# Routing the first half of the tokens inside the last two attention groups of an AdaLN, attention and mixture-of-experts kernel

## The chip, the cores and the metric

The kernel runs on one core of one Trainium2 chip. The metric is the device time of one execution in microseconds (us), lower is better. The kernel before has a median of 799.03 us over 3 runs (798.55 to 799.05).

## What is computed

The input is 4 batches of 1024 tokens with 128 features (float32). One transformer block with adaptive layer norm runs over it:

```python
h = _layernorm(x) * (1 + ca) + sa
x = x + ga * attention(h)          # 16 heads of 8, rope, causal, softmax, output projection
h = _layernorm(x) * (1 + cb) + sb
shared_out = _expert(h, sg, su, sd)              # silu(h @ g.T) * (h @ u.T), then d
probs = softmax(h @ wr.T + rb)                   # 7 routed experts
scores, idx = top_k(probs, 2); scores = scores / scores.sum()
out = shared_out + sum_e w[..., e] * _expert(h, rg[e], ru[e], rd[e])
x = x + gb * out
```

The inner width of an expert is 352. The shifts, scales and gates (sa, ca, ga, sb, cb, gb) come from a small product per batch.

## The kernel before

**Tiling.** Tokens are handled as 32 tiles of 128, as 8 chunks n of 512 (4 tiles each, two chunks to a batch), and as two halves g of 4 chunks (2 batches). Attention runs in 16 groups ("quads", NQ = 16) of 4 heads of one batch; quads 12 to 15 are the last batch's. Each quad has 10 steps (STEPS), and a step has 3 slots (SLOTS), so 30 slots. In a step TensorE computes two pairs of scores (L1681), ScalarE takes their exp (L973, ACT), GpSimd (POOL) masks diagonal tiles (L775), and TensorE multiplies with the values two steps later (L1658).

**The ring.** Everything else that TensorE writes during attention goes through three PSUM banks in an order written out by `quad_pieces`: a list of entries, each with a slot, that TensorE writes (`ring_write`) after the score pair of that slot and VectorE (DVE) or ScalarE reads and frees (`ring_item`), strictly in this order on both sides. An entry waits until the entry three places ahead of it is freed. Kinds: row maxima of later quads ("masked", "plain", "left"), "shift" (the transposed row maxima of quad n + 1, which go by ScalarE, GpSimd and a DMA of SyncE into quad n + 1's operands), "norm" (transposed outputs of a half quad, normalised by VectorE), and in quads 14 and 15 "turn" and "project": the transposed attention output of a chunk of batches 0 to 2, copied to SBUF, and its output projection, which VectorE adds to the residual and takes the layer norm's statistics of. Quad 14 does chunks 0 to 3 from slot 9 on, quad 15 chunks 4 and 5 from slot 2 on. Row maxima of later quads end in quad 14.

**Behind attention.** The last batch's chunks 6 and 7 are turned and projected (L1710, L1766). Then, for each chunk, ScalarE normalises (L1001), TensorE turns the rows (L1722), ScalarE modulates them twice (`modulate2`: a float32 copy for the router and a high part, L1011 and L1014), VectorE subtracts the low part (`second2`, L1293), TensorE multiplies with the router (L1728) and VectorE adds the bias (`logits`). GpSimd (chunks 0 to 3) or VectorE (4 to 7) modulates the unturned rows (`modulate_rows`), which are what is scattered later. For each half VectorE then does the routing: `softmax_shift`, exp on ScalarE (`exp7`), `softmax_scale`, `ranks`, `weights`, a product on TensorE that counts (`counts`, L1736), `prefix`, `starts`, `slots`, `experts`: some 60 small operations, each waiting for the one before it (L1311 to L1400).

**Shared expert.** For each chunk TensorE computes gate and up in three pieces of the inner width (128, 128, 96; `gate_up`, L1750, 6 matmuls of 512 columns each), ScalarE takes silu (L1030), VectorE the product (`hidden`, L1416), TensorE the down product (`down`, L1758), VectorE adds it to the residual (`shared_sum`, L1420). A gate-and-up piece may be written when the hidden product two pieces ahead of it is done. The weights of the 7 routed experts are loaded and split meanwhile into a high part (`first_part`, ScalarE, L1019) and a low part (`second_part`, VectorE, L1425), through two buffers: load e waits for the low part of e - 2. The order of all this is written out per engine, and VectorE's order puts the routing steps of a half between the hidden products.

**Routed tiles.** GpSimd scatters each row to its two slots in DRAM by indirect DMA (L782, 64 in all, 32 for each half, the second half's first 8 before its tile loop and the others one by one in it). A half has 38 slot tiles of 128 rows of one expert, 76 in all. SyncE loads them (L638), TensorE transposes (L1831), computes gate and up of the tile's expert (L1843), transposes (L1864) and computes down (L1854); the parts of four tiles are in flight (`slot_step`). GpSimd scatters the result by indirect DMA (L844). TensorE begins with them when the shared expert is done and all weights are split. At the end the two results of each token are read back, added, gated and stored.

The waits at the head of the first turned rows and of the first scatters before:

```python
pe.wait_ge(s_ring_free, len(BY_DVE))             # turn_normalised(n), n < 2: attention's ring is all free
pool.wait_ge(s_hid, len(IC) + 1 + x // 2)        # scatter x of the first half paced by hidden products
```

## Time and profile before

| what | value |
|---|---|
| median of 3 runs | 799.03 us |
| profiled execution | 797.6 us, its span 795.9 us |
| busy: PE / DVE / ACT / POOL | 686.8 / 573.4 / 545.9 / 342.0 us |
| granted TensorE clock, mean | 0.947 of full |
| chain that ended last, by engine | PE 59%, DVE 18%, ACT 9%, issue 7%, DMA 3% |

The span is the time between the first and the last instruction of the profiled execution. Busy times overlap; a busy time near the length of a stretch names the engine that bounds that stretch. "PE" is TensorE's matmuls, "PEld" its weight loads. The chain of waits is followed back from the last instruction to what released each step. Positions are us from the start of the span. Attention's last two groups run from 436 to 489 us, the transition and the shared expert to 594.7, the routed tiles to 772, the rest is reading back and storing.

### The profile page before, as it was taken

What the parts mean: (1) busy time and instruction counts of PE and PEld (TensorE: products, weight loads), DVE (VectorE), ACT (ScalarE), POOL (GpSimd) and SP (SyncE); (2) the same over time, 40 slices, a digit from 0 to 9 for tenths busy, and PEclk for the clock granted to TensorE, in tenths of its full rate; (3) what the DMA queues carried; (4) which work ended last, traced back from release to release, by engine and by line L of the source; (5) the groups of instructions that cost most, each with busy time, mean ns of one, the idle gap of its engine ahead of it and who ended that gap; (6) DMA issues with size and microseconds to landing.
All of it is one profiled execution on the core that took longest, in us unless ns stands there. A gap on an engine that the chain in (4) does not pass through costs nothing.

```text
span 795.9 us, 18082 instructions
## 1 busy us (share of the span) xinstructions
PE 686.8 (86%) x5304; PEld 395.3 (50%) x5304; DVE 573.4 (72%) x2042; ACT 545.9 (69%) x1013; POOL 342.0 (43%) x551
## 2 busy tenths in 40 slices
PE   2986899999999999999999986678869989999970
PEld 1553123333333333333333434567659889999960
DVE  5797889999999999999999834574773323333543
ACT  2785259889989888989888788544325556666640
POOL 1367613232322322232322123235657887666652
PEclk9999569999999999999999999699999999999995
DMA  9246021111111111111110079202233322223425
GB/s 260 83 156 219 1 74 47 39 30 29 47 47 48 47 28 30 41 46 47 48 37 14 1 136 178 68 23 81 63 92 78 82 76 81 66 68 104 131 87 158
DMA packets 64760, 59.46 MB, mean 75 GB/s; under 512 B 10798, under 2 KB 52398, under 8 KB 64668
## 3 DMA queue, kind: packets, MB, share of 16 engines
q1 hardware_dynamic: 58924, 46.85, 23.3%
q0 software_dynamic: 4480, 9.64, 3.4%
q10 hardware_dynamic: 1264, 1.84, 0.7%
q8 instruction: 46, 0.75, 0.4%
q14 instruction: 46, 0.38, 0.2%
HBM read 33.57 MB, written 24.33 MB: 73 GB/s over the span
## 4 chain that ended last, share of the span: by engine, by line
PE 59%; DVE 18%; ACT 9%; issue 7%; DMA 3%; POOL 1%; SPq 1%; ACTq 1%; DVEq 0%; POOLq 0%
PE ps L1658 13%; PE ps L1602 10%; PE ps L1843 9%; PE ps L1681 7%; PE ps L1854 6%; DVE junk L1238 5%; ACT probs L973 5%; PE ps L1864 3%; PE ps L1758 2%; PE ps L1636 2%; DVE junk L1210 2%; PE ps L1750 2%; DMA routed_results_scratch<-y_s,s_dest 1%; PE ps L1831 1%; DVE rot L1193 1%
## 5 line engine op out<-in xcount | busy, mean ns | idle before, releaser
L973 ACT ACTIVATE probs<-ps 128x1024 f32<-128x1024 f32 (+1 forms) x320 | 285.5, 941 | 34.5 <-PE ps L1681 32.1
L1210 DVE CUSTOM_DVE_ANT_0 junk<-ps,tri 128x512 f32<-128x512 f32 (+3 forms) x512 | 218.5, 487 | 13.9 <-PE ps L1602 11.6
L1602 PE MATMUL ps<-ka,qa 61*128 61x256 bf16 (+3 forms) x788 | 186.7, 325 | 10.0 <-DVE rowmax L1210 3.0
L775 POOL TENSOR_SCALAR_AFFINE_SELECT probs<-probs 128x512 f32<-128x512 f32 x128 | 79.7, 634 | 191.8 <-ACT probs L973 191.8
L1658 PE MATMUL ps<-probs,v 128*32 128x512 f32 (+3 forms) x1536 | 157.7, 498 | 1.3 <-POOL probs L775 1.1
L1681 PE MATMUL ps<-qa,ka 64*128 64x512 bf16 (+3 forms) x768 | 144.6, 331 | 7.7 <-ACT probs L973 5.6
L1602 PEld LDWEIGHTS ps<-ka,qa 61*128 61x128 bf16 x788 | 53.0, 95 | 159.8 <-DVE rowmax L1210 80.4
L844 POOL DMA_INDIRECT routed_results_scratch<-y_s,s_dest x76 | 76.2, 1003 | 41.0 <-issue 35.0
L782 POOL DMA_INDIRECT slot_rows_scratch<-rows,slot x64 | 64.1, 1001 | 56.6 <-DVE slot L1393 30.1
L1243 DVE TENSOR_REDUCE leftmax<-ps 128x1 f32<-128x512 f32 x120 | 78.4, 686 | 8.5 <-PE ps L1602 8.5
L1532 DVE TENSOR_TENSOR hid_s<-sg,ps 128x352 f32<-128x352 f32 x76 | 39.6, 521 | 46.2 <-ACT sg L1087 46.0
L1854 PE MATMUL ps<-wd,hidT 128*128 (+1 forms) x456 | 64.3, 277 | 5.8 <-ACT hidT L1105 5.8
L1525 DVE TENSOR_TENSOR h_lo<-ps,h_hi 128x128 fp32r<-128x128 f32 x76 | 22.2, 291 | 59.7 <-ACT h_hi L1080 59.3
L1854 PEld LDWEIGHTS ps<-wd,hidT 128*128 128x128 f32 (+1 forms) x456 | 60.6, 192 | 7.4 <-issue 7.3
L1658 PEld LDWEIGHTS ps<-probs,v 128*32 128x32 f32 x1536 | 33.8, 108 | 54.5 <-issue 49.3
L1681 PEld LDWEIGHTS ps<-qa,ka 64*128 64x128 bf16 x768 | 42.5, 94 | 33.4 <-ACT probs L973 21.2
L1087 ACT ACTIVATE sg<-ps 128x352 f32<-128x352 f32 x76 | 35.2, 463 | 33.8 <-PE ps L1843 32.0
L1096 ACT ACTIVATE y_s<-ps,s_weight 128x128 f32<-128x128 f32 x76 | 27.9, 367 | 33.5 <-PE ps L1854 25.4
L1238 DVE CUSTOM_DVE_ANT_0 junk<-ps,above 128x256 f32<-128x256 f32 x136 | 49.3, 419 | 0.0
L749 POOL TENSOR_TENSOR mrest<-mneg,mparts 32x128 f32<-32x128 f32 x16 | 6.7, 417 | 92.7 <-ACT mparts L936 92.7
L1843 PE MATMUL ps<-w_hi,h_hi 128*128 x152 | 45.3, 380 | 1.2 <-issue 1.1
L1210 DVE DVE_READ_ACCUMULATOR2_ANT rowmax<- 128x1 f32 x512 | 42.6, 83 | 0.1
(195 smaller groups left out, 1168.4 us busy)
## 6 DMA issues: line engine op xcount, KB each, us to landing
slot_rows_scratch<-cst SPq DMA_DIRECT2D x1, 5396.0 KB, 36.1
srow<-slot_rows_scratch SPq DMA_DIRECT2D x76, 71.0 KB
k_parts_scratch<-qk_parts SPq DMA_DIRECT2D x12, 320.0 KB, 2.7
ka<-k_parts_scratch SPq DMA_DIRECT2D x32, 120.0 KB
q_parts_scratch<-qk_parts SPq DMA_DIRECT2D x12, 256.0 KB, 2.6
qa<-q_parts_scratch SPq DMA_DIRECT2D x32, 96.0 KB
ka<-k_parts_scratch SPq DMA_DIRECT2D x32, 80.0 KB
xs<-in_x SPq DMA_DIRECT2D x4, 512.0 KB, 9.4
```

The source lines that it names most:

```text
L775: nc.gpsimd.affine_select(out=p, in_=p, compare_op=ALU.is_ge, fill=0.0, base=0, pattern=[[0, HQ], [1, T]], channel_multiplier=-1).then_inc ...
L782: nc.gpsimd.indirect_dma_start(slot_d, bass.IndirectOffsetOnAxis(ap=slot[:, k, t:t + 1], axis=0), rows[:, t, :], None).then_inc(s_scatter[ ...
L844: nc.gpsimd.indirect_dma_start(y_d, bass.IndirectOffsetOnAxis(ap=s_dest[:, d:d + 1], axis=0), y_s[:, j, :], None).then_inc(s_y_out[j], 16)
L973: nc.scalar.activation(probs[(n * NS + s) % 4][:, 2 * h:2 * h + 2, 0:UNTIL[s] - FROM[s]], ps[:, 2 * h:2 * h + 2, FROM[s]:UNTIL[s]], ACT.Ex ...
L1210: last = V.tensor_tensor_reduce(out=junk[:, bank - 5, at:at + w], in0=ps[:, bank, at:at + w], in1=tri[:, CH - w:CH], scale=1.0, scalar=LOW ...
L1238: last = V.tensor_tensor_reduce(out=junk[:, bank - 5, cols], in0=ps[:, bank, cols], in1=above[:, h, q - CG, :], scale=1.0, scalar=LOW, op0 ...
L1243: last = V.reduce_max(leftmax[m][:, row, q - CG:q - CG + 1], ps[:, bank, :], AX.X)
L1602: last = MM(ps[:, bank, at:at + w], qa[m][g0:g0 + KS, c0 + q * T:c0 + (q + 1) * T], ka[m][g0:g0 + KS, d0 + k0:d0 + k0 + w], start=True, st ...
L1658: last = MM(ps[VW * h:VW * (h + 1), 4, q0:CH], v4[m][:, k, h, :], probs[(n * NS + s) % 4][:, h, p0:p0 + CH - q0], start=begins, stop=ends ...
L1681: last = MM(ps[:, 2 * pair + g, at:at + CH - q0], ka[m][g * HG:(g + 1) * HG, pair * KW + kb * T:pair * KW + (kb + 1) * T], qa[m][g * HG:(g ...
L1843: last = MM(ps[:, 1 + 2 * t2 + g, 0:NI], ht[:, t2, :], wt[:, bass.ds(e, 1), g, :], start=(k == 0), stop=(k == 2))
L1854: last = MM(ps[:, 6, 0:D], hidT[0:w, t2, c, :], wd[0:w, bass.ds(e, 1), c, :], start=(c == 0), stop=(c == len(IC) - 1))
```

## The change

The entries of `quad_pieces` for quads 14 and 15 are now two tables. In quad 14 the turns and projections of chunks 0 to 3 go to slots 19 to 29. VectorE then takes the variance of half 0 (16 tiles; before, of 24 tiles behind attention) and normalises its 16 tiles itself, with a square root that ScalarE takes at step 2 of quad 15 (`deviation(0)`). In quad 15 three new kinds of entries route half 0: "rows" (transposed rows, modulated by VectorE into hT), "router" (logits) and "counts"; VectorE does `softmax_shift`, `softmax_scale`, comparisons, `ranks`, `weights`, `prefix`, `starts`, `slots` and `experts` between and at these entries, ScalarE the exp at step 7. Turns and projections of chunks 4 and 5 move to slots 17 to 22. GpSimd modulates the rows of half 0 at steps 5 and 6 of quad 15.

Behind attention the rows of chunks 0 to 3 are turned after their modulation, so ScalarE only copies the high part. The shared expert begins when the last batch's residual is added. Half 1 is routed later in VectorE's order, in pieces of a generator between the hidden products of chunks 4 to 7, with the four `modulate_rows` of half 1 among them; `shared_sum(4)`, `(5)` and `(6)` now stand right behind the first hidden product of chunks 5, 6 and 7. Down of chunk 3 and router 7 stand ahead of gate and up of chunk 4. Second-half scatters: 12 ahead of the tile loop instead of 8; the first half's are not paced any more. All loops over slot tiles are written out, and the first half's results are read back three loads earlier.

```diff
+FIRST_HALF = [(19, "turn", 0), (20, "turn", 1), (21, "project", 0), (23, "turn", 2), (24, "project", 1),
+              (26, "turn", 3), (27, "project", 2), (29, "project", 3)]
+SECOND_HALF = [(9, "rows", 0), (10, "rows", 1), (11, "router", 0), (12, "rows", 2), (13, "router", 1), (14, "rows", 3),
+               (15, "router", 2), (16, "router", 3), (17, "turn", 4), (18, "turn", 5), (20, "project", 4), (22, "project", 5),
+               (28, "counts", 0)]
-    units = {NQ - 2: range(4), NQ - 1: range(4, 2 * (B - 1))}.get(n, ())
...
+    late = {NQ - 2: FIRST_HALF, NQ - 1: SECOND_HALF}.get(n, ())
+    plan += [(slot, kind, n, None, u) for slot, kind, u in late]
...
+        AHEAD = 12
+        ROWS_TURNED = {u: slot for slot, kind, u in SECOND_HALF if kind == "rows"}
...
                 for s, tiles in enumerate(STEPS):
+                    for u in range(GC) if n == NQ - 1 else ():
+                        if s == (ROWS_TURNED[u] // SLOTS) + 2:
+                            modulate_rows(u)
...
-                pool.wait_ge(s_hid, len(IC) + 1 + x // 2)
...
+                    if s == 2 and n == NQ - 1:
+                        deviation(0)
+                    if s == 7 and n == NQ - 1:
+                        exp7(0)
...
+                if n < GC:
+                    nc.scalar.activation(h2_hi[:, n * CH:(n + 1) * CH], ps[:, TURN[u], :], ACT.Copy).then_inc(s_h2_hi, 1)
+                    return
...
             normalise(7)
             first_part(1)
+            first_part(2)
             silu(3)
             modulate2(7)
-            first_part(2)
+            first_part(3)
+            exp7(1)
             silu(4)
-            exp7(1)
-            first_part(3)
+            first_part(4)
             silu(5)
-            first_part(4)
+            first_part(5)
             silu(6)
-            first_part(5)
+            first_part(6)
             silu(7)
-            first_part(6)
...
+                elif kind == "counts":
+                    incl = prefix(0, bank)
+                    end = starts(0, incl)
+                    slots(0, incl, bank)
+                    dve.sem_inc(s_ring_free, 1)
+                    experts(0, end)
...
+            for x in range(len(RING_PIECES)):
+                ring_item(x)
+                done = RING_PIECES[x][1:]
+                if done == ("project", NQ - 2, None, GC - 1):
+                    variance(GTILES[0], s_var2)
+                    scale2(0)
+                    dve.wait_ge(s_v4, NQ)
+                    for n in range(GC):
+                        normalise(n)
+                elif done == ("router", NQ - 1, None, GC - 1):
+                    V.memset(beats[:], 0.0).then_inc(s_beats, 1)
+                    softmax_shift(0)
+                elif done == ("project", NQ - 1, None, GC):
+                    softmax_scale(0)
+                    dve.wait_ge(s_beats, 1)
+                    beaten(0, range(NE))
+                elif done == ("project", NQ - 1, None, GC + 1):
+                    ranks(0)
+                    weights(0)
...
+            def route_second():
+                softmax_scale(1)
+                yield
+                beaten(1, range(4))
+                yield
+                beaten(1, range(4, NE))
+                yield
+                ranks(1)
+                yield
+                weights(1)
+                modulate_rows(4)
+                yield
+                modulate_rows(5)
+                incl = prefix(1, GROUPED)
+                yield
+                modulate_rows(6)
+                end = starts(1, incl)
+                yield
+                modulate_rows(7)
+                yield
+                slots(1, incl, GROUPED)
+                yield
+                experts(1, end)
+                yield
+                yield
...
             softmax_shift(1)
             second2(7)
+            shared_sum(3)
+            next(routing)
+            hidden(4, 0)
+            next(routing)
+            hidden(4, 1)
+            next(routing)
+            next(routing)
+            hidden(4, 2)
+            next(routing)
             hidden(5, 0)
-            modulate_rows(7)
+            shared_sum(4)
+            next(routing)
             hidden(5, 1)
-            softmax_scale(1)
-            ranks(1)
+            next(routing)
             hidden(5, 2)
-            shared_sum(4)
-            weights(1)
+            next(routing)
             hidden(6, 0)
-            second_part(3)
-            incl = prefix(1)
+            shared_sum(5)
+            next(routing)
             hidden(6, 1)
-            end = starts(1, incl)
+            second_part(4)
             hidden(6, 2)
-            shared_sum(5)
-            slots(1, incl)
+            next(routing)
             hidden(7, 0)
-            second_part(4)
-            experts(1, end)
+            next(routing)
+            shared_sum(6)
             hidden(7, 1)
             second_part(5)
             hidden(7, 2)
-            shared_sum(6)
             second_part(6)
             shared_sum(7)
...
-            turn_normalised(7)
-            gate_up(4)
+            turn_rows(7)
             down(3)
             router(7)
+            gate_up(4)
             gate_up(5)
             down(4)
-            counts(1)
+            pe.wait_ge(s_sel, GRP)
+            group_counts(1, GROUPED).then_inc(s_prefix, 1)
```

## Rows read from the trace of the kernel before

**Rows 1.** Busy time by stretch: stretch, length, then busy us (xinstructions) per engine, granted clock.

```profile
463.48:483.60 20.12, 18.45 (x172) 7.58 (x176) 6.57 (x23) 17.18 (x21) 3.88 (x7) 1.00 1.09 199
502.90:529.90 27.00, 18.21 (x90) 14.57 (x90) 20.01 (x74) 11.35 (x21) 3.11 (x4) 0.82 0.01 4
547.50:594.70 47.20, 38.61 (x241) 32.71 (x239) 34.04 (x94) 15.46 (x23) 26.62 (x27) 0.97 0.27 79
```

**Rows 2.** TensorE's timeline, last attention group: start, us, line, form [idle before, releaser].

```profile
463.48 0.61 PE L1681 MATMUL ps<-qa,ka 64*128 64x512 bf16 x4 [1.68 <-DMA qa<-mparts]
465.01 0.66 PE L1621 MATMUL ps<-eye,xn 128*128 128x128 f32 x4
...
473.77 1.16 PE L1627 MATMUL ps<-wo_gated,oT 128*128 128x128 f32 x8
```

**Rows 3.** ScalarE's timeline, last attention group: step 2, step 7, table load.

```profile
467.81 1.94 ACT L973 ACTIVATE probs<-ps 128x1024 f32<-128x1024 f32 x2
...
479.82 1.02 ACT L973 ACTIVATE probs<-ps 128x1024 f32<-128x1024 f32 x1 [0.72 <-PE ps L1681]
...
484.98 1.28 ACT L995 ACT_TABLE_LOAD   x1
```

**Rows 4.** VectorE's timeline: eight normalisations at the start, the last norm.

```profile
10.09 2.14 DVE L1165 TENSOR_SCALAR xn<-xs,mean,rstd 128x128 f32<-128x128 f32 x8
...
489.40 0.29 DVE L1263 TENSOR_TENSOR xn<-ps,recip 128x128 f32<-128x128 f32 x1
```

**Rows 5.** VectorE's busy time in each step of the second half's routing.

```profile
567.95:571.87 3.92, 3.73 (x18) 1.00 0.16 56
573.07:574.46 1.39, 1.27 (x6) 1.00 0.12 33
576.07:578.08 2.01, 1.85 (x11) 1.00 0.42 102
578.68:580.70 2.02, 1.77 (x12) 1.00 0.12 42
581.90:585.05 3.15, 2.81 (x13) 1.00 0.00 0
586.48:587.47 0.99, 0.92 (x4) 1.00 0.29 90
```

**Rows 6.** Chain of waits through the shared expert: start, us, what.

```profile
503.07 4.31 PE ps L1750 x12
...
515.47 2.87 PE ps L1750 x6
...
528.82 0.79 PE ps L1728 x8
...
531.59 1.35 ACT rows L1001 x4
...
547.69 4.04 PE ps L1758 x24
...
566.03 0.70 DVE rows L1406
...
585.82 1.63 PE ps L1750 x6
587.44 2.69 PE ps L1758 x24
```

**Rows 7.** Timeline of GpSimd and VectorE where their passes overlap.

```profile
495.33 1.18 POOL L793 TENSOR_TENSOR rows<-rows,mod_rows 128x512 f32<-128x512 f32 x1 [0.18 <-POOL rows L789]
495.50 1.04 DVE L1132 TENSOR_TENSOR part_a<-stats 128x8 f32<-128x8 f32 x1
```

**Rows 8.** GpSimd's timeline: two result scatters, 19 tile steps apart.

```profile
604.45 1.00 POOL L844 DMA_INDIRECT routed_results_scratch<-y_s,s_dest  x1 [1.62 <-issue]
...
657.04 1.00 POOL L844 DMA_INDIRECT routed_results_scratch<-y_s,s_dest  x1 [0.16 <-issue]
```

**Rows 9.** TensorE's busy time and matmuls of L1843 in a stretch of routed tiles.

```profile
662.00:733.00 71.00, 40.57 (x199) 31.36 (x200) 1.00 0.24 69
```

393 lines of the change are left out of this document (175 added, 218 removed).

## The prediction

> **What bounds the kernel now.** I read the busy time by stage first [rows 1], then the timelines of the engines in the last attention group [rows 2 to 4], the chain of waits through the shared expert [rows 6], and GpSimd's timeline and TensorE's pace in the routed tiles [rows 8, 9]. Four stretches matter. (a) The last attention group's score window is full for two engines: of 20.1 us TensorE is busy 18.5 and ScalarE 17.2, VectorE only 6.6 [rows 1]. (b) Attention ends at 489.69 us, when VectorE has normalised the last output [rows 4]; I call this t0. (c) From 502.9 to 529.9 VectorE is the bound (20.0 of 27 us): it does the first half's routing between the pieces of the shared expert, and TensorE sits idle 6.8 us before the piece at 515.47 [rows 1, 6]. (d) From T = 547.5, the end of chunk 3's gate and up products, to 594.7, the end of the shared expert, TensorE is busy 38.6 of 47.2 us [rows 1]. The routed tiles follow: GpSimd paces the first ones, TensorE the others [rows 8, 9]. The change takes work out of (c), puts it into (a), and reorders (d).
>
> **Prices.** Four transposes 0.6 us, a projection 1.1 [rows 2], a router 0.8, a gate-and-up piece 1.45 (its row of 1.63 runs to the last drain), a down product 2.7, a VectorE pass over 128x512 0.6 to 0.7 [rows 6]. One sixteenth of normalise on VectorE 0.26 (eight in 2.14, rows 4). A table switch on ScalarE 1.28 [rows 3]. Routing of one half on VectorE: scale, comparisons and ranks 3.9, weights 1.35, prefix 2.0, starts 2.0, slots 3.15, experts 1.0 [rows 5].
>
> **Part 1, group 14 (next to last).** The turns and projections move behind the transposition of the next group's row maxima. That shift then starts some 3.4 us earlier and 3.4 us more of TensorE work lies behind it, so the 1.68 us wait for its DMA [rows 2] is covered. TensorE is otherwise full, its work is the same: **-1.7 us**.
>
> **Part 2, group 15 (last).** I count from its first scores (463.48 before). Before, the second steps' exps end at 6.3 [rows 3] and t0 is at 26.2. After:
> - ScalarE's step 2 ends at about 5.7; then table load and square root to 7.2. VectorE scales to 7.7 and normalises 16 tiles to 11.9 (16 x 0.26), all before it takes any further ring entry. TensorE has reached slot 9 at about 5.4 and waits there for the first four tiles, to 8.9; behind this wait in its queue stand score pair 1 of step 3 and so ScalarE. ScalarE has to load the exp table again (1.28).
> - The first router needs VectorE's modulated copy, which stands behind the 16 tiles: 12.7.
> - From there TensorE has score pairs, value products, 4 more transposition and router entries, turns 4 and 5 and projections 4 and 5, and is the bound: adding entry after entry, step 5 starts at 17.6, step 6 at 21.4, step 7 at 24.5, step 7's exps end at 26.8 (before: 17.4, rows 3).
> - Only then ScalarE does the router's exp (27.1), which VectorE waits for: scale and comparisons to 29.7, then the norm and projection entries held up behind them (0.6 + 1.5) to 31.8, ranks 33.0, weights 34.3. TensorE waits for the ranks with its counts product at slot 28, and the last three value products (3 x 1.0) stand behind it: 33.8 to 36.8, copy and transposes to 38.1. VectorE does prefix, starts, slots and experts (8.15) to 42.4, and only then the last norm: t0 at 43.0.
> So t0 comes 43.0 - 26.2 = **+16.8 us** later. The lower bound needs no TensorE queue at all: the chain behind step 7's exps (the router's exp 0.3, then 3.9 + 2.1 + 1.35 + 8.15 + 0.6 = 16.1 of VectorE) starts no earlier than 17.4 + 2.6 for the two table loads, which gives 36 and +10.
>
> GpSimd's modulation of the first half (8 passes of 1.18) runs from about 9.6 to 20 in this group; its own masks are needed later, cost none. But a VectorE pass of two SBUF operands that began under such a pass took 1.04 us where its like takes 0.2, and ended with GpSimd's [rows 7]. Whether normalise, with one SBUF operand, waits too is not in the trace: between 0 (it is not held) and 4.0 us (its last 8 tiles held until GpSimd's first four passes are over, and the first router with them). I take **+2.0**, the middle, since only a pass of another kind shows it.
> The Trainium skill (GPSIMD Engine Reference, Key points) says that GpSimd contends with VectorE instructions of two SBUF inputs or in a 2-port mode. The trace agrees for the first kind (1.04 us against 0.2). By that rule the term would be 4.0 and the time 2 us more than I give.
> The Trainium skill (ScalarE: Activation LUTs, What ACT_TABLE_LOAD costs) gives about 2.66 us for each change of set, load and drain, and tells to group calls by set, which speaks against a square root between exps. The trace shows the load, 1.28, right behind the last exp, with no gap for a drain. By the page the stretch would be 2.8 us longer and the sum some 2 us more.
>
> **Part 3, from t0 to chunk 2.** Before: 40.2 us (489.69 to 529.9). After, from t0: turns of the last batch to 1.15, first two row turns to 2.35, projections to 4.4, and VectorE's two low parts and two residual sums to 6.2: gate and up of chunk 0 start at 6.2 instead of 13.4 [rows 6]. Their first two pieces take 4.3 as before (half clock at first). Silu's table is in place at 9.8, the first hidden product at 11.1, the third piece runs at 11.15 without the 6.8 us wait. Then ScalarE is next: it normalises chunk 4 (1.64; the chain shows 1.35 of such a step, rows 6) before row turn 4, to 15.1, and has modulation and normalise again ahead of chunk 1's silu, to 18.8. Down of chunk 0 ends at 24.2, router 25.0, chunk 2 starts at 25.65: **-14.5 us**.
> Chunks 2 and 3 keep their pace, 17.6 us before; one more weight split (0.8) ahead of chunk 3's silu, a 0.4 us slow clock less: **+0.4**.
>
> **Part 4, from T to the end of the shared expert (before 47.2).** Gate and up of chunk 4 now come behind down of chunk 3 and its router: start T + 7.6 instead of T + 5.3. The four modulations of rows (1.4 each; only one was in this stretch) and all routing of the second half go between the pieces, and three residual sums are placed ahead of hidden products: VectorE waits there for a down product that TensorE issues only after the piece released by the hidden product before. From T: hidden (4,0) 11.3, (4,1) 12.85, (4,2) 15.5 behind the ranks, (5,0) 18.8 behind weights and a modulation; piece and down to 23.0; sum, modulation, prefix, (5,1) 27.6; modulation and starts, (5,2) 31.5; (6,0) 33.5; piece and down to 37.7; sum and slots (3.15), (6,1) 42.1. The last expert weights are loaded only after the split that follows (43.0), and ScalarE converts them ahead of chunk 7's silu: (7,0) at about 48.7. Piece and down to 52.85, sum, two hiddens and a split 55.6, down and sum 59.3. So 59.3 - 47.2 = **+12.1 us**. It is a chain of VectorE and TensorE in turns; the DMA in it I took as 3 to 4 us.
>
> **Part 5, routed tiles.** GpSimd scatters 12 second-half tiles ahead instead of 8 (15.1 us from T + 41.5, over at T + 56.6; this is covered by 2.7 us, and each us beyond would count in full), so 20 instead of 24 ride in its tile loop. Before, 19 steps ran at (657.04 - 604.45) / 19 = 2.77 us while a tile of TensorE, six such matmuls, takes 71.0 x 6 / 199 = 2.14 [rows 8, 9]. Four steps fewer x 0.63: **-2.5 us**. Unrolled loads, the read of results three tiles earlier, the order of allocations and the unpaced first scatters (40 us, over long before their rows are read): 0, since the same queues do the same bytes; -1 to +2 for where the result read collides.
>
> **Sum.** -1.7 + 16.8 + 2.0 - 14.5 + 0.4 + 12.1 - 2.5 = +12.6. Span 795.9 + 12.6 = 808.5; the profiled run was 797.6, so 1.7 lies around the span: 810.2. The median of the runs is 1.4 above the profiled one; I forecast **811**. Bounds of the terms: part 2 from +10 to +21, part 4 from +6 to +15.
>
> **Rivals.**
> *Not slower after all (0.13), about 791.* VectorE's idle time in group 15 (13.5 of 20.1 us) takes the routing in, so that the group grows only by TensorE's added entries (6.5 us less the 1.6 idle, 4.9), and half of part 4 overlaps: -1.7 + 4.9 - 14.5 + 6 - 2.5 = -7.8. For it: that idle time. Against it: order. It decides at one place, the router's exp behind step 7; the routing tail would have to end before ScalarE's last copy.
> *A draw (0.07), about 799:* the same, with part 2 at its lower bound of +10 and part 4 at +6.
> *Half clock in part 4 (0.17), about 823.* TensorE would be busy about 25 of the 46 us from T + 13 on. The piece at 515.47, behind 6.8 us of idleness, took 2.87 against 1.63, and a down product at 547.69 took 4.04 against 2.69 [rows 6]. Seven such pieces and three downs on the chain: 7 x 1.24 + 3 x 1.35 = 12.7 more. Against it: the piece at 585.82, which also stood behind a wait for a hidden product, ran at full clock [rows 6].
> *My forecast* has 0.63. The change does what it says, since all of it is program order; the only thing outside is the padding write, whose start does not move back.
>
> **Range and chances.** What this kernel's measurement can tell from no change is about 0.2%, 1.6 us. Forecast's bounds and part of the half-clock case: 800 to 823. Faster 0.12, same 0.07, slower 0.81.
>
> **What would show it.** Right: in the last group ScalarE has two more table loads, TensorE a gap of over 3 us ended by VectorE's normalise, and one ended by the ranks; t0 near 505; no gap of 6.8 us in chunk 0; chunk 2 some 26 us behind t0; gaps of 3 to 4.5 us in chunks 5 to 7, ended by hidden products; shared end near 608. Wrong: t0 before 498 (part 2's queue is not the bound), or less than 52 us from T to the end (part 4 overlaps).

## The result, and the profile after

| | kernel before | kernel after |
|---|---|---|
| median (4 runs each) | 798.79 us | 827.14 us (822.93 to 827.50) |
| ratio to before | | 1.0344, 95% interval 1.0310 to 1.0378 |
| span of the profiled execution | 795.9 us | 825.2 us |
| granted TensorE clock, mean | 0.947 | 0.923 |

The change makes the kernel 28 us slower. The direction is the one forecast, the size is 16 us above the 811 and 4 us above the range's end of 823.

The page of the kernel after, its head, two engines' busy time and the granted clock in 40 slices:

```profile
span 825.2 us, 17955 instructions
...
PE 704.4 (85%) x5320; PEld 405.4 (49%) x5320; DVE 584.2 (71%) x2062; ACT 538.6 (65%) x994; POOL 341.7 (41%) x550
...
PEclk9997579999999999999999958799887999999995
```

Before, TensorE was busy 686.8 us. Now it is busy 17.6 us longer for 16 more matmuls: the same work at a lower clock, and the clock row shows where, in slices 24 to 26 and 29 to 31 (of 20.6 us each): the last attention group, the stretch behind it and the second half of the shared expert.

The stretches of the prediction, as windows of the kernel after (start:end, length, busy time of each engine with its number of instructions, granted clock, DMA share, GB/s). They run from the last group's first scores to t0, to gate and up of chunk 2, to T, to the end of the shared expert, to the end:

```profile
core 0: us, PE busy (x) PEld busy (x) DVE busy (x) ACT busy (x) POOL busy (x), PEclk, DMA share, GB/s
462.19:516.84 54.65, 37.68 (x257) 19.14 (x256) 34.69 (x117) 22.56 (x27) 16.42 (x19) 0.78 0.67 112
516.84:543.86 27.02, 21.78 (x117) 18.18 (x117) 11.80 (x33) 14.12 (x25) 20.62 (x22) 0.81 0.36 107
543.86:562.46 18.60, 13.41 (x75) 10.68 (x74) 7.62 (x12) 10.52 (x20) 9.33 (x10) 0.97 0.21 62
562.46:626.42 63.96, 46.23 (x241) 38.01 (x239) 35.00 (x96) 14.66 (x22) 16.19 (x22) 0.82 0.14 43
626.42:825.20 198.78, 168.50 (x1216) 162.30 (x1216) 76.36 (x173) 108.91 (x380) 125.21 (x243) 0.93 0.32 91
```

Against before, term by term:

| stretch | before | after | difference | forecast |
|---|---|---|---|---|
| up to the last group's first scores | 463.48 | 462.19 | -1.3 | -1.7 |
| last group, to t0 | 26.2 | 54.65 | +28.4 | +18.8 |
| t0 to gate and up of chunk 2 | 40.2 | 27.0 | -13.2 | -14.5 |
| chunk 2 to T | 17.6 | 18.6 | +1.0 | +0.4 |
| T to the end of the shared expert | 47.15 | 63.96 | +16.8 | +12.1 |
| routed tiles to the end | 201.3 | 198.8 | -2.5 | -2.5 |
| sum | | | +29.2 | +12.6 |

Two terms carry the miss: +9.6 in the last group and +4.7 from T on. The others are off by 2.3 in all.

TensorE's timeline in the last group of the kernel after, the lines ahead of which it stood idle for over 2 us and some of the routers (start, length, line, output and inputs, count, idle time before and what ended it):

```profile
471.88 0.63 PE L1664 MATMUL ps<-eye,rows 128*128 128x128 f32 x4 [3.73 <-DVE rows L1403]
...
479.45 1.84 PE L1668 MATMUL ps<-wr,hT 128*128 128x7 f32 x8 [4.37 <-DVE hT L1230]
...
484.20 1.87 PE L1668 MATMUL ps<-wr,hT 128*128 128x7 f32 x8
...
490.81 1.06 PE L1668 MATMUL ps<-wr,hT 128*128 128x7 f32 x8
...
506.61 1.14 PE L1635 MATMUL ps<-sel,cst 128*128 128x112 f32 x4 [2.46 <-DVE sel L1310]
...
516.90 1.97 PE L1753 MATMUL ps<-eye,xn 128*128 128x128 f32 x8 [3.83 <-DVE xn L1249]
```

VectorE's and then GpSimd's lines beside them. VectorE's sixteen normalising operations take 7.96 us, not 4.2, and GpSimd's first passes of modulation lie under them:

```profile
470.62 7.96 DVE L1403 TENSOR_SCALAR rows<-xs,mean,rstd 128x128 f32<-128x128 f32 x16 [0.15 <-DVE nbias L1121]
```

```profile
472.69 1.19 POOL L746 TENSOR_TENSOR rows<-rows,mod_rows 128x512 f32<-128x512 f32 x1 [2.86 <-PE ps L1664]
474.06 1.28 POOL L750 TENSOR_TENSOR rows<-rows,mod_rows 128x512 f32<-128x512 f32 x1 [0.18 <-POOL rows L746]
475.31 1.23 POOL L746 TENSOR_TENSOR rows<-rows,mod_rows 128x512 f32<-128x512 f32 x1
```

ScalarE's, from the third step's exps on, shows the chain's head: exps to 468.45, then the square root with its two table loads, then VectorE:

```profile
466.51 1.94 ACT L955 ACTIVATE probs<-ps 128x1024 f32<-128x1024 f32 x2
468.47 1.28 ACT L931 ACT_TABLE_LOAD   x1
469.76 0.21 ACT L931 ACTIVATE rstd<-rstd 128x16 f32<-128x16 f32 x1
469.99 1.28 ACT L955 ACT_TABLE_LOAD   x1
```

From T on, some of TensorE's waits for hidden products, and the last down product, which took 5.49 us where the four ahead of it took 2.84 each:

```profile
591.55 0.50 PE L1786 MATMUL ps<-h_hi,ws_hi 128*128 128x512 f32 x1 [4.22 <-DVE hid L1389]
...
607.24 0.80 PE L1786 MATMUL ps<-h_hi,ws_hi 128*128 128x512 f32 x1 [4.53 <-DVE hid L1389]
...
614.59 2.84 PE L1794 MATMUL ps<-wds_gated,hid 128*128 128x128 f32 x24
...
620.20 5.49 PE L1794 MATMUL ps<-wds_gated,hid 128*128 128x128 f32 x24 [2.77 <-DVE hid L1389]
```

and VectorE's residual sums in the same stretch, placed behind the first hidden product of the next chunk; each waits for a down product that TensorE issues only behind the next piece (a third such sum, at 617.47, waits 4.39 us):

```profile
586.94 0.69 DVE L1393 TENSOR_TENSOR xs<-xs,ps 128x512 f32<-128x512 f32 x1 [4.39 <-PE ps L1794]
...
602.75 0.69 DVE L1393 TENSOR_TENSOR xs<-xs,ps 128x512 f32<-128x512 f32 x1 [5.38 <-PE ps L1794]
```

### The profile page after: what moved, and what is told of

Read it like the earlier page. It is cut to its first block and busy times, and to the rows that moved or that the text cites. A ratio compares the mean times of both kernels' runs of the same rounds, so it can differ in the third digit from the quotient of the medians.

```text
span 825.2 us, 17955 instructions
## 1 busy us (share of the span) xinstructions
PE 704.4 (85%) x5320; PEld 405.4 (49%) x5320; DVE 584.2 (71%) x2062; ACT 538.6 (65%) x994; POOL 341.7 (41%) x550
## 3 DMA queue, kind: packets, MB, share of 16 engines
q10 hardware_dynamic: 1264, 1.84, 0.7%
## 5 line engine op out<-in xcount | busy, mean ns | idle before, releaser
L955 ACT ACTIVATE probs<-ps 128x1024 f32<-128x1024 f32 (+1 forms) x320 | 285.5, 940 | 49.5 <-PE ps L1724 47.2
L1183 DVE CUSTOM_DVE_ANT_0 junk<-ps,tri 128x512 f32<-128x512 f32 (+3 forms) x512 | 218.4, 487 | 14.1 <-PE ps L1627 11.8
L1701 PE MATMUL ps<-probs,v 128*32 128x512 f32 (+3 forms) x1536 | 160.4, 507 | 0.3 <-ACT outT L943 0.3
L1724 PE MATMUL ps<-qa,ka 64*128 64x512 bf16 (+3 forms) x768 | 146.3, 334 | 6.6 <-ACT probs L955 6.3
L1701 PEld LDWEIGHTS ps<-probs,v 128*32 128x32 f32 x1536 | 34.2, 110 | 55.0 <-issue 50.7
L1786 PE MATMUL ps<-h_hi,ws_hi 128*128 128x512 f32 (+1 forms) x48 | 23.4, 488 | 22.4 <-DVE hid L1389 21.3
```

Of the source, the lines that this page charges most:

```text
L955: nc.scalar.activation(probs[(n * NS + s) % 4][:, 2 * h:2 * h + 2, 0:UNTIL[s] - FROM[s]], ps[:, 2 * h:2 * h + 2, FROM[s]:UNTIL[s]], ACT.Ex ...
L1183: last = V.tensor_tensor_reduce(out=junk[:, bank - 5, at:at + w], in0=ps[:, bank, at:at + w], in1=tri[:, CH - w:CH], scale=1.0, scalar=LOW ...
L1701: last = MM(ps[VW * h:VW * (h + 1), 4, q0:CH], v4[m][:, k, h, :], probs[(n * NS + s) % 4][:, h, p0:p0 + CH - q0], start=begins, stop=ends ...
L1724: last = MM(ps[:, 2 * pair + g, at:at + CH - q0], ka[m][g * HG:(g + 1) * HG, pair * KW + kb * T:pair * KW + (kb + 1) * T], qa[m][g * HG:(g ...
```

## The experiments

My theory after the result: in the last group, (a) GpSimd's modulation slows VectorE's normalising, (b) TensorE idles ahead of the rows and then runs at half clock, (c) the routing's tail (`starts`, `slots`, `experts`) delays the last norm; from T on, (d) the place of the residual sums. "Last group" below is from its first scores to t0 in each kernel's own trace.

The runs were taken in groups, and each group has its own measure of the kernel before. For e1 to e8, e17 and e18 that took 799 to 800 us. For e9 to e16 it took 833 to 835 us, and those are compared only among themselves and by stretches of the last group. There is no trace of the kernel before from these. The record gives the chip of each group by a number, and number 8 stands beside 833 and 834 us (e9 to e13) as well as beside 799 us (e17 and e18), so whether the 833 us belong to a chip or to a time is open.

### e1: TensorE kept busy

```diff
+                    keep_busy(m, bank, 14 if what == 0 else 0)   # ahead of the wait for rows 0
...
+                    keep_busy(m, bank, 18 if what == 0 else 0)   # ahead of the wait for router 0
```

The 32 extra matmuls write into a bank that the next entry overwrites; nothing of the computation is left out.

> The changed kernel with 32 matmuls added whose results nobody reads: 14 ahead of the wait for the first normalised rows and 18 ahead of the first router, each of 512 columns into the bank that the entry behind them overwrites. They fill the two idle times of TensorE (3.7 and 4.4 us) in the last group. Theory clock: these idle times bring the granted clock to half, which costs some 7 us in the group (a router takes 1.8 us where it took 0.8). Then routers ahead of step 6 take 0.8 to 1.0 us, the end of attention comes some 7 us earlier and the time is 819 to 822. Rival: VectorE's queue sets the group's end and the slow matmuls are hidden behind it: the matmuls run faster, but the time stays within 2 us of 827, or rises by as much as the added matmuls overrun the gaps.

Median 825.59 us (819.85 to 827.66), ratio 1.0342 [1.0318, 1.0365]. TensorE's lines ahead of the first router, profiled execution:

```profile
466.12 3.18 PE L1641 MATMUL ps<-qa,ka 64*128 64x512 bf16 x14
...
472.17 4.05 PE L1641 MATMUL ps<-qa,ka 64*128 64x512 bf16 x18
...
477.50 1.06 PE L1674 MATMUL ps<-wr,hT 128*128 128x7 f32 x8 [1.27 <-DVE hT L1230]
```

In this execution, the fastest of four, routers take 1.06 and the last group 48.6 us in place of 54.65. The stretch from the first router to the first scores of step 6 holds the same 80 matmuls in both kernels, and TensorE is busy through all of it. In the kernel after, and in e1:

```profile
479.45:493.70 14.25, 14.25 (x80) 9.53 (x81) 4.61 (x12) 4.70 (x5) 4.72 (x4) 0.62 1.15 180
```

```profile
477.50:486.93 9.43, 9.43 (x80) 6.52 (x81) 4.60 (x12) 4.69 (x5) 4.74 (x4) 1.00 1.17 173
```

So the lower clock costs 4.8 us in this stretch, with contention and square root as they were, and e1's group is 6.0 us shorter in all. As a cure the filling isn't shown: the median of 825.59 is the rival's, within 2 us of 827. The time follows the mean clock from execution to execution, with the filling (819.85 us at 0.940, 827.66 at 0.925) and without it (the kernel after: 822.93 at 0.934, 827.50 at 0.924). So the runs show what the half clock costs, not what brings it.

### e2: GpSimd's modulation behind the normalising

```diff
+                pool.wait_ge(s_xn2, GC)
                 pool.wait_ge(s_ring, RING_INDEX["rows", NQ - 1, None, n] + 1)
```

> The changed kernel with one wait more: GpSimd begins to modulate the first half's rows in the last group only when VectorE has normalised all 16 tiles. Theory contention: GpSimd's passes hold VectorE's normalisation (8.0 us for what takes 4.2). Then the 16 tiles take 4.2 us, the first router starts 3.8 us earlier, and TensorE's second idle time shrinks to under 1 us: time 823 if the clock falls all the same, down to 816 if it stays full. Rival: normalise is slow for a reason of its own (two engines and a write of strided rows): its 16 tiles still take about 8 us, and the time is 827 or more.

Median 819.05 us (815.51 to 826.10), ratio 1.0236 [1.0189, 1.0284]. VectorE's line:

```profile
470.85 4.19 DVE L1404 TENSOR_SCALAR rows<-xs,mean,rstd 128x128 f32<-128x128 f32 x16 [0.15 <-DVE nbias L1122]
```

Normalising takes 4.19 us, so (a) holds: the contention costs 3.8 us. The median fell by 8.1 us and lies within the theory's 816 to 823. The profiled execution, though, was the slowest of four and kept routers of 1.84 and 1.87, all four of them, and its last group is only 1.9 us shorter: its trace shows the shorter normalising and not where the median's 8 us come from.

### e3: the routing's tail behind the last norm

```diff
-                    end = starts(0, incl)
-                    slots(0, incl, bank)
...
-                    experts(0, end)
...
+            end = starts(0, kept[0])      # behind the last norm
+            experts(0, end)
...
+            slots(0, kept[0], None)       # behind hidden(0, 1)
```

> The changed kernel with the end of the first half's routing moved on VectorE: starts and experts stand behind the last norm of attention, slots behind the second hidden product of chunk 0; only prefix and a copy of the counts stay ahead of the last norm. Theory queue: the last norm stands behind 8 us of routing and TensorE waits for it, so attention ends about 6 us earlier and the time is about 821 to 822.5 (some of the moved 6 us lands on the chain of chunk 0). Rival: the work is only moved and VectorE bounds the next stage as well: the time stays within 1.5 us of 827.

Median 822.68 us, ratio 1.0285 [1.0245, 1.0325]; last group 51.1 us, 3.6 shorter, and t0 to the first down product 21.7 in place of 23.1. So (c) is worth some 4.5 us, about what the theory gave (821 to 822.5). The intervals of e3 and of the kernel after (1.0310 to 1.0378) overlap a little, so the size is rough; the shorter group stands in the trace.

### e4 and e6: residual sums later, and 8 scatters ahead

```diff
             hidden(5, 0)
-            shared_sum(4)
...
             hidden(5, 2)
+            shared_sum(4)
```

and likewise sums 5 and 6 behind `hidden(6, 2)` and `hidden(7, 2)`. Prefix, starts, slots and the last modulation of rows move back with the sums, by one or two hidden products; they stay in this stretch. e6 is e4 with `AHEAD = 8`.

> The changed kernel with VectorE's order in chunks 5 to 7 altered: the residual sums of chunks 4, 5 and 6 stand behind the third hidden product of the next chunk, as before, and prefix behind the sum of chunk 4; the routing steps and row modulations are the same and stay in this stretch. Theory order: three times VectorE waits 4.4 to 5.4 us for a down product while TensorE waits for VectorE's hidden product, so of the stretch from chunk 3 to the end of the shared expert (63.9 us, 47.2 before) 9 to 12 us go: time 815 to 819. Rival: the stretch is long because there is more routing in it and because of TensorE's half clock: it shrinks by 3 us at most, time 824 or more.

> The kernel with VectorE's sums of the shared expert's chunks 4 to 6 behind the third hidden product of the next chunk, now with 8 in place of 12 tiles of first results laid down ahead of the routed weights. Theory (the routed stage was 5 us longer in that kernel since the 12 scatters end later than the shared expert): the routed stage is back at 199 to 201 us, the shared expert's second half stays at 46 to 48 us, and the time is 808 to 811 us. Rival (the routed stage begins with the table of weights and destinations, which depends on the routing's last steps, not on the scatters): the routed stage stays at 203 to 204 us and the time at 813.

e4: median 813.49 us, ratio 1.0183 [1.0147, 1.0220]. The window from T to the end of its shared expert:

```profile
562.50:609.00 46.50, 38.13 (x239) 32.03 (x238) 34.72 (x95) 14.34 (x22) 7.94 (x8) 0.98 0.16 48
```

46.5 us in place of 63.96: (d), the order of VectorE's steps with the sums at its head, is the whole +16.8 of this stretch, more than the 9 to 12 us expected. The sums now wait 0.55 us, not at all and 1.37 us in place of 4.39, 5.38 and 4.39. TensorE's busy time fell by 8.1 us (38.13 against 46.23, clock 0.98 against 0.82) and its idle time by 9.4 (8.4 against 17.7): the waits, and the lower clock that came with them, in about equal parts. Some 5 us came back in the routed tiles (203.7 against 198.8), since the twelve scatters, the first at 598.93, ended at 614.31, behind the shared expert's end at 608.6, and the table of weights and destinations came only then (GpSimd):

```profile
613.35 0.96 POOL L782 DMA_INDIRECT slot_rows_scratch<-rows,slot  x1 [0.30 <-issue]
614.32 0.20 POOL L808 COPY s_weight<-srow 128x1 f32 x1
```

e6: median 811.24 us (810.48 to 817.04), routed tiles 202.1. The gain of 2 us lies inside the spread of both, and 202.1 lies between the theory's 199 to 201 and the rival's 203 to 204, so the scatters' part stays undecided.

### e5: no contention, and the first idle stretch filled

e2's edit and e1's first 14 matmuls.

> The kernel after with two things in its last attention group: GpSimd's modulation of the rows begins only behind VectorE's sixteen normalising operations, and 14 extra matmuls of 512 columns are issued ahead of the wait for the first rows (their results are overwritten; nothing of the computation is left out). Theory (the half clock in the last group follows TensorE's idle stretch of 3.7 us ahead of the rows; that and the collision of VectorE with GpSimd are the missing 10 us): normalising takes 4.2 us, the first router matmuls 0.8 to 1.1 us in place of 1.87, the last group to the end of its last normalisation 44 to 46 us in place of 54.7, and the time 815 to 818 us. Rival (the clock falls there for another reason than that one idle stretch): routers still at 1.8, the group at 51 to 53, and 819 to 826 us as without the extra matmuls.

Median 824.29 us (820.22 to 826.66). Routers 1.83 and 1.87 in spite of it, last group 49.5:

```profile
470.86 0.66 PE L1670 MATMUL ps<-eye,rows 128*128 128x128 f32 x4 [0.63 <-DVE rows L1404]
...
474.74 1.83 PE L1675 MATMUL ps<-wr,hT 128*128 128x7 f32 x8 [1.57 <-DVE hT L1231]
```

Filling the 3.7 us does not keep the clock: behind waits of 0.63 and 1.57 us TensorE ran its routers at half clock for some 10 us. The rival holds in the routers and the time, and as a cure the filling falls; the group is between the two forecasts (44 to 46, and 51 to 53). That its median is 5 us above e2's is not explained; their intervals, 1.0271 to 1.0360 and 1.0189 to 1.0284, overlap.

### e7 and e8: the costs undone together

e7 is e2, e3 and e6 in one, with `second_part(4)` and `(5)` one step earlier. e8 moves on top of that the turns and projections of chunks 4 and 5 ahead of the rows. VectorE then normalises behind the residual sum of chunk 5 and takes the routing's steps from scale to weights behind the first norm, and ScalarE takes the router's exp at step 6:

```diff
-SECOND_HALF = [(9, "rows", 0),
...
+SECOND_HALF = [(0, "turn", 4), (1, "turn", 5), (2, "project", 4), (4, "project", 5), (9, "rows", 0),
...
```

> The kernel after with four things set right at once: GpSimd's modulation behind the normalising; the first half's starts and experts behind the last normalisation and its slots behind the shared expert's first hidden product; VectorE's sums of chunks 4 to 6 later, with the gated products of chunks 4 and 5 one step earlier; 8 scatters ahead in place of 12. Theory (the costs stand in different stages and add): minus 4 to 8, minus 4, minus 14 and minus 3 us from 827 give 796 to 800 us. Rival (what is saved in the last group is given back as idle TensorE and a lower granted clock in the shared expert, since each stage then waits for VectorE): 803 to 810 us.

> As the kernel with the four things set right, and in the last attention group TensorE turns and projects tiles 4 and 5 in its first slots, ahead of the first half's rows, while the softmax, comparisons and ranks of the first half come on VectorE behind the last tile's normalisation. Theory (VectorE's work of the routing's first steps stood between the last group's start and the end of its normalisation, and TensorE's idle stretch ahead of the rows is filled with work that was to be done anyhow): the last group takes 33 to 40 us in place of 54.7, and the time is 788 to 795 us, under the kernel before. Rival (the routing's steps only move behind the normalisation, where counts and the shared expert's hidden values wait for VectorE): 796 to 803 us, no better than the kernel with four things alone.

e7: median 799.31 us (10 runs), ratio 1.0027 [1.0004, 1.0051]. The singles had saved 8, 4.5 and 13.7 us, e6's scatters 2; together they save 28, so they add, and the theory's 796 to 800 holds. The windows of e7's last group and of its stretch from T on:

```profile
460.88:503.87 42.99, 33.25 (x257) 16.21 (x256) 25.68 (x93) 22.55 (x27) 14.80 (x17) 0.88 0.89 143
549.00:596.03 47.03, 38.91 (x241) 32.73 (x239) 35.46 (x96) 14.65 (x22) 17.69 (x20) 0.96 0.22 64
```

The last group is still 16.8 us above before's 26.2, and what is won behind it (some 13 us up to chunk 2) no more than pays for that: with these costs gone, the change is a draw.

e8: median 798.03 us (10 runs), ratio 0.9981 [0.9968, 0.9994], last group 40.2. That is 0.2% under the before of its own group. e18 below, the same kernel with its scatters paced, has the same median and a ratio of 0.9995, so a gain over before isn't shown. It is the rival's time rather than the 788 to 795 of the theory: TensorE's idle stretch ahead of the rows stayed (3.74 us, rows at 474.67), since the exps and the square root behind them moved back with the projections.

### e9 to e16: where the square root stands

```diff
                 for s in range(NS):
+                    if s == 1 and n == NQ - 1:
+                        deviation(0)
...
-                    if s == 2 and n == NQ - 1:
-                        deviation(0)
```

e10, e11 and e15 are the kernel after with this edit alone, e16 adds e2's, e12 is e7 with it, e9 and e13 are e8 with it, and e14 is the kernel after itself on the same chip as e15 and e16.

> The kernel with projections first, with ScalarE's square root for the first half's normalisation ahead of the second step's exps of the last group (in its idle stretch of 3.0 us) in place of behind the third step's. Theory (with the square root there, VectorE normalises right behind the residual sum of tile 5, some 4 us earlier, and TensorE's idle stretch of 3.74 us ahead of the rows and the half clock behind it go): normalising starts near 469.5 in place of 473.4, routers at 1.06 or less, the last normalisation 3 to 5 us earlier, the time 793 to 796 us, under the kernel before by 0.4% or more. Rival (the two table loads delay the exps that TensorE's value products wait for, or the group is bound by TensorE alone): the last normalisation at most 1 us earlier, the time 797 to 799.

> The kernel after with this one edit: ScalarE's square root for the first half's normalisation ahead of the second step's exps of the last group in place of behind the third step's. Theory (what came on top of the prediction in the last group is a chain from this square root through normalising to the rows, the idle TensorE ahead of them and its half clock): normalising starts 2.5 to 3.5 us earlier, the idle stretch ahead of the rows shrinks from 3.7 to under 1.5 us, the last normalisation comes 3 to 6 us earlier, and the time is 820 to 824 us. Rival (GpSimd's modulation and the queue behind the routing's steps set the group's end whatever the square root does): the last normalisation 0 to 2 us earlier and the time at 824 to 827.

> The same edit of the kernel after as before (square root ahead of the second step's exps), once more since the earlier run's chip showed pauses of ScalarE of up to 12 us in the shared expert. Theory (the 9.8 us that its trace of the last group shows are gained in the time too): the last group 44 to 47 us, the time 816 to 820 us where before takes 799, or the ratio to the kernel before 1.021 to 1.027. Rival (TensorE's half clock falls elsewhere in that group or in the shared expert and gives it back): 822 to 826 us, ratio 1.029 to 1.034.

> The kernel with four things set right (modulation later, routing's tail behind the last normalisation, sums later, 8 scatters ahead), and the square root ahead of the second step's exps. Theory (normalising starts 3 to 4 us earlier, and the last group was bound from there): the last normalisation 3 to 4 us earlier than in that kernel, the ratio to the kernel before 0.994 to 0.998, under before. Rival (with the contention gone, the square root's place is no longer what binds the group, and the two table loads delay the exps instead): ratio 1.000 to 1.004, as without the edit.

> The kernel with the projections of tiles 4 and 5 first and the square root ahead of the second step's exps, once more, beside the others on one chip. Theory of the first trace of it (TensorE idles 0.2, 0.75 and 1.57 us in place of 3.74, yet runs at half clock over 477 to 490, which takes back what was gained): the last group 42 to 44 us, the ratio to before 1.000 to 1.006. Rival (that half clock was one execution's): the last group 37 to 39 us and a ratio of 0.992 to 0.996.

> The kernel after itself, as the measure for the two kernels beside it on the same chip. If this is a chip on which the kernel before takes 799 us: 823 to 828 us, last group 53 to 55 us. If it is the one on which before takes 833: the pauses of ScalarE in the shared expert are those of that chip, not of the square root's place, so the trace shows them here too, and the time is 880 to 885 us (the 874 with the square root earlier, plus up to 10); if they come from the square root's place, it is below 865.

> The kernel after with the square root ahead of the second step's exps. Theory (the last group's 9.9 us arrive in the time): 7 to 10 us below the kernel after on the same chip. Rival (half clock or waits in the shared expert give them back): 0 to 4 us below it.

> The kernel after with the square root ahead of the second step's exps and GpSimd's modulation behind the normalising. Theory (normalising collides with GpSimd only for 0.8 us once the square root is early, 4.98 against 4.19 us, so the two edits remove one and the same cost): 0 to 1.5 us below the kernel with the square root alone. Rival (the costs add): 4 to 8 us below it.

| kernel | median | ratio to before | last group |
|---|---|---|---|
| e14, after | 886.10 us | 1.0628 [1.0607, 1.0648] | 54.55 |
| e15, square root early | 873.74 | 1.0472 [1.0448, 1.0495] | 44.6 |
| e10, e11, the same | 873.39, 874.01 | 1.0496, 1.0466 | 44.8, 44.7 |
| e16, and no contention | 874.22 | 1.0474 [1.0451, 1.0497] | 43.4 |
| e12, e7 with it | 853.71 | 1.0245 [1.0199, 1.0292] | 42.7 |
| e9, e13, e8 with it | 854.56, 855.69 | 1.0263, 1.0238 | 43.6, 41.9 |

Against e14, this one edit takes 9.96 us off the last group, and they arrive: the median falls by 12.4 us (the profiled spans, 882.1 and 871.7, differ by 10.4). That is more than the theory's 7 to 10 and far from the rival's 0 to 4. e10 and e11 show the same group; their times, expected for a before of 799 us, decide nothing. The last group of e14 and of e15:

```profile
461.03:515.58 54.55, 37.67 (x257) 19.29 (x256) 34.71 (x117) 22.56 (x27) 16.52 (x19) 0.78 0.65 113
```

```profile
460.94:505.53 44.59, 35.13 (x257) 16.60 (x256) 31.82 (x117) 22.55 (x27) 16.30 (x19) 0.84 0.77 138
```

Of the 10 us, 2.5 are TensorE's busy time (clock 0.78 to 0.84) and 7.4 its idle time. VectorE and the first router in e15:

```profile
465.55 4.98 DVE L1403 TENSOR_SCALAR rows<-xs,mean,rstd 128x128 f32<-128x128 f32 x16 [0.15 <-DVE nbias L1121]
```

```profile
466.86 1.08 PE L1724 MATMUL ps<-qa,ka 64*128 64x384 bf16 x8 [2.15 <-ACT probs L957]
...
471.46 0.66 PE L1664 MATMUL ps<-eye,rows 128*128 128x128 f32 x4
```

Normalising starts 3.8 us earlier in the group (4.6 in place of 8.4 behind the first scores) and is over at 470.53, before GpSimd's modulation starts at 471.40, so nothing collides but one masking pass of 0.80 us. TensorE never waits for the rows; it waits 2.15 us for the delayed exps instead. e16 confirms it: with e2's edit too, normalising takes the same 4.98 us and the time stays (874.22 against 873.74), so the two edits remove one and the same contention, as the theory of e16 had it. In e12 the edit gives 0.3 us (42.7 against e7's 43.0), and on e8 it makes the group longer (43.6 and 41.9 against 40.2), with two or three of the four routers at 1.84 to 1.88, though TensorE's longest wait ahead of them was 1.57 us. For the last group the theories of e9 and e12 fell and their rivals hold; e13's theory for it (42 to 44 us) is nearly met. How the times of e12, e9 and e13 would stand to e7 and e8 side by side wasn't measured.

The traces of e9 to e16 show something that the others don't: with the 32 scatters of the first half under way, ScalarE and VectorE stop for up to 22 us (e13) with nothing in the trace that ends the stop. ScalarE in e14, the first two silu of the shared expert, which in the kernel after ran without a wait:

```profile
545.29 0.60 ACT L1010 ACTIVATE sgs<-ps 128x512 f32<-128x512 f32 x1 [8.45 <-remote]
...
557.23 0.60 ACT L1010 ACTIVATE sgs<-ps 128x512 f32<-128x512 f32 x1 [11.33 <-remote]
```

They come without the square root's edit too, so they aren't its doing, as e14's expectation had it for a before of 833 us (its 886.10 lies 1 us above the 880 to 885 given). "remote" is what the trace prints where it finds no releaser. From t0 to T, e14 takes 74.9 us where the kernel after takes 45.6: about half of the 57 us between their spans. What makes the engines stop is open.

### e17 and e18: the scatters paced again

```diff
                 if t == 0:
                     pool.wait_ge(s_slot, k + 1)
+                pool.wait_ge(s_hid, len(IC) + 1 + x // 2)
```

> The kernel after with the first half's scatters paced again by the hidden products, as in the kernel before. If the step 'unpaced scatters cost nothing' was right: where the kernel before takes 799 us the time is that of the kernel after, 823 to 828 us (ratio 1.031 to 1.037); where it takes 833 us the pauses of ScalarE stay and the ratio is 1.060 to 1.065. Rival (32 scatters in one go keep instructions or data of the other engines waiting): the pauses in the shared expert's first chunks shrink or move, and the ratio falls below 1.05 on such a chip, or by 2 us or more on the other kind.

> The kernel with the projections first and the three costs undone, with the first half's scatters paced again. If unpaced scatters cost nothing: ratio to the kernel before 0.997 to 1.000 where that takes 799 us, as without the pacing, and 1.02 to 1.027 where it takes 833. Rival: ratio below 1.01 on a chip of the second kind, and 0.990 to 0.996 on one of the first.

e17 (the kernel after with it): 825.39 us, ratio 1.0335 [1.0318, 1.0352]. e18 (e8 with it): 798.03 us (12 runs), ratio 0.9995 [0.9973, 1.0016]. No gain where before takes 799 us: the prediction's zero for the unpaced scatters holds there. No paced run was taken where before takes 833 us, so whether the pauses go with the pacing stays open.

## Why the prediction was right and wrong

**Right: direction and the balance.** Part 1 (-1.7, measured -1.3), part 3 (-14.5, -13.2), chunks 2 and 3 (+0.4, +1.0) and part 5 (-2.5, -2.5) hold within 1.3 us each. For part 5 no run isolates the reason given, the four scatters fewer in the loop, so there only the number is shown. The main argument, that the last group takes up the routing end to end behind step 7's exps and the tail ahead of the last norm, is what the trace shows: TensorE waits 2.46 us for the ranks and 3.83 us for the last norm. "Not slower after all" (0.13) decides where the prediction put it, at the router's exp, which comes 38.1 us behind the first scores. The draw (0.07) is reached only with the costs undone (e7). Of what was named as a sign of error, "t0 before 498" and "less than 52 us", neither came.

**Wrong: the size of part 2.** Against its own positions, counted from the first scores:

| | forecast | after | e1's trace | e15 |
|---|---|---|---|---|
| normalising starts, ends | 7.7, 11.9 | 8.4, 16.4 | 8.4, 16.4 | 4.6, 9.6 |
| first router | 12.7 | 17.3 | 17.2 | 11.7 |
| first scores of step 6 | 21.4 | 31.5 | 26.6 | 21.9 |
| t0 | 43.0, and 2.0 for the contention | 54.65 | 48.6 | 44.6 |

Of the 11.65 us between 43.0 and 54.65, 4.6 stand ahead of the first router. 3.8 of them are the contention, for which I had taken the middle of 0 and 4.0 where the upper end was true; the rest is mostly the square root, 0.7 us later than forecast. Another 5.5 come between router and step 6, for which I had 8.7 us and the kernel needs 14.25. e1's trace, with the same order at full clock, needs 9.43: so 4.8 of the 5.5 are the half clock, and 0.7 my sum of TensorE's entries. The last 1.55 are spread behind it, and 1.1 of them are gone in e1's trace too. In all, by these two traces, the half clock is worth 6.0 us and the contention 1.8 more than the 2.0 that I gave it: 7.8 of part 2's miss of 9.65.

The step that failed is that I priced a half clock as a rival of part 4 only. In part 2 I wrote down a TensorE wait of 3.5 us (to 8.9; it was 3.73) and went on at the full-speed prices of rows 2, though rows 6 show a piece of 2.87 us in place of 1.63 behind a long wait. That this wait brought the half clock isn't shown: e7's trace has the same 3.73 us and routers at full clock, and e5's has only short waits and slow ones. What makes the clock fall stays open. e15's t0 lies near the forecast's 45.0, but by another course: its normalising starts 3.1 us ahead of the forecast's.

**The contention.** Normalising took 7.96 us under GpSimd's passes and 4.19 without them (e2). This is an operation with one SBUF operand of 128 columns; the Trainium skill (GPSIMD Engine Reference, Key points) names VectorE instructions of two SBUF inputs or in a 2-port mode. By that rule, as the prediction read it for this operation, the term was 4.0: the trace agrees, with 3.8, and so does the sum that the prediction gave beside its own. In which mode the operation ran no trace shows.

**The table loads.** Square root and two loads took 468.47 to 471.27, 2.8 us, with the first load right behind the last exp. The Trainium skill (ScalarE: Activation LUTs, What ACT_TABLE_LOAD costs) gives about 2.66 us for each switch, which would make it 5.5; the measurement decides, and 1.28 a load was the right price. The Trainium skill's advice to group calls by table set (ScalarE: Activation LUTs, Table sets: the hidden batching unit) bears here all the same: the two loads cost ScalarE 2.6 us, but the place of the square root cost 10 us in the group, 3.0 of them contention. I counted the delay of VectorE by them and didn't ask what the same root would do ahead of the second step's exps.

**Part 4: right chain, clock left out.** From T, hidden products (4,0), (5,0), (6,0) and (7,0) were forecast at 11.3, 18.8, 33.5 and 48.7 and start at 11.8, 19.4, 34.2 and 49.9. Up to there the chain of residual sum, hidden product and piece is as worked out, 0.5 to 1.2 us late, and e4 shows that the order with the sums ahead is all of it. Of the 4.7 us above the forecast the other 3.5 arise behind (7,0); 2.6 of them are the last down product at half clock (5.49 us against 2.84). The rival "half clock in part 4" (0.17, +12.7) is half true: TensorE's busy time from T on rose from 38.6 to 46.2 us, but (7,0) stood only 1.2 us late, so of these 7.6 us little more than the last down product shows in the length of the stretch. The row at 585.82, which I held against it, was one piece behind one wait.

**The range.** With both of its upper bounds (part 2 at +21, part 4 at +15) the sum is -1.7 + 21 - 14.5 + 0.4 + 15 - 2.5 = +17.7, which gives 817; the end of 823 came from the half-clock rival of part 4. The measured +28.4 lies outside part 2's own bound of +21: that bound held the whole contention and nothing for the clock. Two figures don't follow from the prediction's own terms either: 810.2 + 1.4 is 811.6, not 811, and t0 by its sum stands at 463.5 - 1.7 + 43.0 + 2.0 = 506.8, where its signs say 505. Neither changes what is said above.

## What to carry to other kernels

When a chain crosses three engines inside a stretch that was full, look for its earliest link and ask what an earlier place would do: here one square root's place in ScalarE's order was worth 10 us, contention and idle TensorE included, and 0.3 us on e7, where the contention was gone and the clock full. A consumer that waits for a producer which the consumer's own output feeds (a residual sum ahead of the hidden product that releases the next piece) cost twice here, 9.4 us as waiting and 8.1 us as lower clock. And where you write down an idle stretch on TensorE, give the matmuls behind it at half speed a price and a chance of their own in every part, not in one; these runs don't tell which stretch will bring it.

## What the runs showed of the hardware

- A VectorE tensor_scalar over 128x128 f32 with one SBUF operand, sixteen in a row: 4.19 us alone (e2), 7.96 under GpSimd tensor_tensor passes of 128x512 (after), 4.98 with a masking pass of GpSimd under it (e15).
- The same 80 matmuls took 14.25 us at a mean granted clock of 0.62 and 9.43 at 1.00, with TensorE busy throughout in both (after and e1).
- The granted clock does not follow from the idle time just before alone: behind 3.73 us of idleness routers took 1.03 in e7's trace, behind 1.57 us they took 1.83 in e5's. In e9's trace TensorE was busy for all of the 13 us from 477 to 490 at a granted clock of 0.50. Executions of one kernel differ with it: e1's four had clocks of 0.925 to 0.940 and times of 827.66 to 819.85 us.
- The same kernel before took 799 us in some groups of runs and 833 to 835 in others, and the change cost 3.4% in the first and 6.3% in the second (e14), where ScalarE and VectorE pause for up to 22 us (e13) while indirect DMAs run. Whether that goes with the chip is open. A ratio found in one group need not hold in the next.
